# TensorE's attention work in a loop over three units, with rings of three, and the final projections of all images as a stage of their own

## The chip, the cores and the metric

The kernel runs on one core of a Trainium2 chip. The metric is device time in microseconds (us) for one execution, the median of several runs. Engines are called as in the profile: PE is TensorE (PEld its weight loads), DVE VectorE, ACT ScalarE, POOL GpSimd, SP SyncE, whose only work here is issuing DMAs. SPq and ACTq are the DMA issues of SP and ACT.

## The reference

The input x has 8 images of 56 x 56 positions with 128 channels, float32. Two residual layers follow one another: `x = x + L0(gn(x))` and `x = x + L1(gn(x))`, where gn is a group norm over 32 groups. L0 is a gated global convolution by FFT; its stages are not touched. L1 works on each position (token) by itself, with 8 heads of 16 channels:

```python
q, k, v = xs @ Wq.T, xs @ Wk.T, 2 * (xs @ Wv.T)          # each n x 8 heads x 16
q, k, v_h = l2norm(q), l2norm(k), l2norm(v)
attn_head = softmax(einsum('bnhd,bngd->bnhg', v_h, v_h))  # 8 x 8 between the heads of a token
q, k = (einsum('bnhg,bngd->bnhd', attn_head, y) for y in (q, k))
attn = softmax(einsum('bnhd,bnhe->bnde', k, q))           # 16 x 16 between channels, over heads
out = einsum('bnhd,bnde->bnhe', v, attn)
out = transpose(out, (0, 3, 1, 2)).reshape(b, n, 128) @ proj_w.T + proj_b
```

The transpose before the last product mixes tokens: row e x 196 + r of its input is channel e of all heads of tokens 16 r to 16 r + 15. So a row of the result draws on 16 tokens, and a block of results on tokens of half an image.

## The kernel before

Six stages run one after another, each a block in which every engine has its own program: load_weights, project_in, make_taps, convolve, project_out, attend. In convolve, project_in and project_out TensorE runs a hardware loop (`Fori`); the body of convolve holds 8 images with 52 matmul calls each (32, 16, 2 and 2) and some ten waits on semaphores each, and is repeated 30 times for 32 chunks. The change is in attend (L1026), whose program is written out in full on all engines.

attend handles the 25088 tokens of all images in 112 units of 224 tokens. Two units are one turn n (448 tokens, 4 blocks of 112). Its pipeline, with the names of the code:

- **SP**: load_xn (L1103) brings the normed input of turn n+3, 128 rows of 1792 B. turn (L1105 to L1118) waits until the unit four turns back has left, then loads the heads of turn n from DRAM scratch: eight DMAs into v_blocks (L1117), each of 896 runs of 32 B, and one into qk_rows (L1118), 3584 runs of 136 B. v_blocks and qk_rows have four buffers of two units each.
- **PE**, in round i: mix(i) (L1177), scores(i+1) (L1162), project of one block (L1146), outputs(i-2) (L1201), logits(i-1) (L1189), a final group if one is due (L1214, L1216), project of a second block. The projections are 8 units ahead of the attention. scores has 28 matmul calls, mix 28, outputs 28, logits 56, a projection 1, a final group 8. One float32 call shows as two matmul and two weight-load records.
- **ACT**: copy_in takes each projected block out of PSUM with two squares and a copy (L1249 to L1251); root makes the norms of a turn (L1255, square root); store_heads writes v_heads and qk_heads to scratch (L1260, 448 runs; L1261); exp_s (L1267) and exp_l (L1273) are the exponentials; leave_mix (L1281, L1282) takes mix out. Square root and exponential need different tables, so each turn has two table loads.
- **DVE**: squares and clamp (L1327, L1331), normalize_q and normalize_kv (L1341 to L1351), among them a small copy of the v norms (L1344), mask (L1358), weigh (L1364, L1369), divide (sum, reciprocal, product: L1375, L1377, L1381), leave (L1389) into oT.
- **POOL**: spreads k_mixed into k_blocks (L1136), one instruction of 1.7 us per unit.

s_exp, e_blocks, q_mixed, k_blocks, p_norm have two buffers. oT holds two images, x1_in one, ps_fin is one bank. The final projections of image b are eight groups (FINS, L1088), placed in rounds (b+1) x 14 + 3 and the seven behind it: PE adds the projection and x1 (by a product with the identity) into ps_fin, DVE adds the bias (L1397), ACT stores 196 KB (L1288) and after the eighth loads the next image's x1, 1568 KB (L1290). So 56 of the 64 groups lie within the 112 rounds, and 8 after them.

```python
            for i in range(ROUNDS):
                bk = AHEAD * BPB + 2 * i
                if unit(i):
                    mix(i)
                if unit(i + 1):
                    scores(i + 1)
```

## Time and profile before

| | before |
|---|---|
| runs | 3313.82 us median of 3 (3308.23 to 3314.02) |
| the profiled execution | 3298.07 us, its span 3296.3 us, mean clock of TensorE 0.952 |
| PE, PEld | 2941.7 us (89%), 2143.9 us (65%) |
| DVE, ACT, POOL | 1875.7 (57%), 1272.4 (39%), 565.2 us (17%) |
| DMA queue of instructions (q8) | 300 packets, 4.92 MB |
| attend | from the first load at 2011 us to the end |

The profile is of one execution. Times in the views are from the start of its span. Busy time counts an engine's instructions, not its waits; matmuls are pipelined and their ends modelled, so single durations of PE overlap and add up to more than the stretch they take, whereas the pieces of the chain don't. PEclk is the clock that TensorE was granted, as a share of full speed. Queue q1 is SP's DMAs, q10 ACT's, q8 the one that brings instructions. An idle time is given with what ended it; "issue" means nothing that the profile shows.

### The profile page before, as it was taken

Reading aid. Unit: us, or ns where it says so; the run is one execution under the profiler, and the core shown is the slowest. Engines: PE = TensorE matmul, PEld = TensorE weight load, DVE = VectorE, ACT = ScalarE, POOL = GpSimd, SP = SyncE. Lnnn points to the kernel's source line nnn. Section 1 sums busy time; section 2 is a strip of 40 time slices with the busy share of each in tenths; the row PEclk is TensorE's granted clock in tenths of the full one; section 3 lists DMA queues with packets and bytes.
Section 4 is the critical chain, followed back from the end, with each engine's and each line's share of the span. In section 5 each row is a group of like instructions: output and inputs, shape, how many; then the busy total and the mean of one; then the engine's idle time right before and its main releaser. Section 6 shows DMA issues by size and latency. Waiting matters only on the chain. (4 is left out here: it accounts for less than half of the span.)

```text
span 3296.3 us, 144029 instructions
## 1 busy us (share of the span) xinstructions
PE 2941.7 (89%) x62769; PEld 2143.9 (65%) x62769; DVE 1875.7 (57%) x3334; ACT 1272.4 (39%) x2841; POOL 565.2 (17%) x419
## 2 busy tenths in 40 slices
PE   5676989999999999999998995888898888888887
PEld 4563369766666666666665442677777777777776
DVE  4452542566666666666664774555555555556553
ACT  3553552422222222222222443554444454444431
POOL 0000030022222222222221112111111111111111
PEclk9888889999999999999999997999999999999999
DMA  5877000022112111121123994655556556555652
GB/s 140 228 231 206 1 1 1 11 47 46 45 44 46 44 45 45 44 46 44 44 46 105 412 383 139 94 85 90 99 100 109 103 89 117 92 107 85 113 87 58
DMA packets 1015825, 318.90 MB, mean 97 GB/s; under 512 B 863345, under 2 KB 1002158, under 8 KB 1010350
## 3 DMA queue, kind: packets, MB, share of 16 engines
q1 hardware_dynamic: 692626, 169.81, 24.9%
q10 hardware_dynamic: 322844, 143.73, 16.0%
q8 instruction: 300, 4.92, 0.6%
q14 instruction: 55, 0.45, 0.0%
HBM read 157.66 MB, written 155.75 MB: 95 GB/s over the span
## 5 line engine op out<-in xcount | busy, mean ns | idle before, releaser
L845 DVE TENSOR_TENSOR terms<-spec,ps_z 112x456 f32<-112x456 f32 x1024 | 575.5, 625 | 403.7 <-PE ps_z L728 403.7
L738 PEld LDWEIGHTS ps_q<-inv_w,prod 112*57 112x57 f32 x16384 | 450.9, 133 | 174.6 <-issue 172.2
L738 PE MATMUL ps_q<-inv_w,prod 112*57 112x56 f32 x16384 | 484.4, 217 | 1.3 <-DVE prod L851 1.3
L826 POOL TENSOR_TENSOR prod<-terms 112x456 f32<-112x456 f32 x256 | 297.7, 1163 | 998.8 <-DVE terms L845 998.8
L728 PE MATMUL ps_z<-x_half,fwd_w 120*112 120x456 f32 x1024 | 458.4, 570 | 0.0
L783 ACT ACTIVATE q_half<-ps_q 121x448 f32<-121x448 f32 x255 | 139.4, 547 | 826.4 <-PE ps_y L746 826.4
L1136 POOL TENSOR_TENSOR k_blocks<-k_mixed,same_of 128x896 f32<-128x896 f32 x112 | 188.2, 1680 | 1045.0 <-ACT k_mixed L1282 1045.0
L1189 PE MATMUL ps_l<-q_mixed,k_blocks 32*64 32x64 f32 x12544 | 229.6, 221 | 88.2 <-issue 87.7
L1189 PEld LDWEIGHTS ps_l<-q_mixed,k_blocks 32*64 32x64 f32 x12544 | 205.4, 133 | 106.1 <-issue 97.9
L1162 PE MATMUL ps_s<-v_blocks 128*64 128x64 f32 x6272 | 229.7, 233 | 18.7 <-issue 13.8
L1201 PEld LDWEIGHTS ps_o<-p_norm,v_blocks 128*64 128x64 f32 x6272 | 195.4, 138 | 70.4 <-issue 64.9
L728 PEld LDWEIGHTS ps_z<-x_half,fwd_w 120*112 120x112 f32 x1024 | 160.4, 176 | 121.9 <-issue 106.1
L1146 PE MATMUL ps_qkv<-weights,xn_in 128*112 128x384 f32 x448 | 212.4, 563 | 28.1 <-DMA xn_in<-x_mid_normed 16.7
L1358 DVE TENSOR_TENSOR e_blocks<-s_exp,same_of 128x896 f32<-128x896 f32 x112 | 123.6, 1104 | 193.4 <-ACT s_exp L1267 193.4
L1162 PEld LDWEIGHTS ps_s<-v_blocks 128*64 128x64 f32 x6272 | 211.4, 147 | 28.5 <-issue 16.5
L1201 PE MATMUL ps_o<-p_norm,v_blocks 128*64 128x64 f32 x6272 | 212.4, 225 | 11.3 <-issue 6.5
L1273 ACT ACTIVATE p_exp<-ps_l 128x448 f32<-128x448 f32 x112 | 61.1, 545 | 368.1 <-PE ps_l L1189 368.1
L720 PEld LDWEIGHTS ps_x<-fwd_h,v_in 56*56 56x56 f32 x8192 | 130.0, 128 | 91.8 <-issue 91.7
L1177 PEld LDWEIGHTS ps_l<-qk_rows,e_blocks 64*64 64x64 f32 x6272 | 116.2, 145 | 103.8 <-issue 99.7
L720 PE MATMUL ps_x<-fwd_h,v_in 56*56 56x57 f32 x8192 | 163.9, 218 | 4.6 <-DMA v_in<-conv_in 3.8
L851 DVE TENSOR_TENSOR prod<-terms 112x456 f32<-112x456 f32 x256 | 162.0, 633 | 8.8
L1375 DVE TENSOR_REDUCE z_sum<-p_exp 128x28 f32<-128x448 f32 x112 | 69.3, 619 | 169.4 <-ACT p_exp L1273 169.1
(135 smaller groups left out, 4315.5 us busy)
## 6 DMA issues: line engine op xcount, KB each, us to landing
qk_heads<-st_qk ACTq DMA_DIRECT2D x56, 476.0 KB, 4.2
qk_rows<-qk_heads SPq DMA_DIRECT2D x56, 476.0 KB, 6.8
conv_in<-v_sb ACTq DMA_DIRECT2D x112, 224.0 KB, 3.3
v_in<-conv_in SPq DMA_DIRECT2D x512, 49.0 KB
conv_out<-y_sb ACTq DMA_DIRECT2D x512, 49.0 KB
y<-conv_out SPq DMA_DIRECT2D x8, 1792.0 KB, 13.4
x_in<-in_x SPq DMA_DIRECT2D x8, 1568.0 KB, 9.4
shortcut<-short ACTq DMA_DIRECT2D x8, 1568.0 KB, 6.3
```

The costliest lines, as they stand in the source:

```text
L720: last = pe.matmul(ps_x[64 * ri:64 * ri + SIDE, r, c * NF:(c + 1) * NF], v_in[b % 2][rows, c * SIDE:(c + 1) * SIDE], k.fwd_h[rows, ri * NF ...
L728: last = pe.matmul(ps_z[b % 2][x][0:NFFT, 0:PC], k.fwd_w[:, x, :], x_half[b % 2][:].rearrange("p r x -> p (r x)"), start=True, stop=True)
L738: last = pe.matmul(ps_q[64 * ri:64 * ri + NF, c * SIDE:(c + 1) * SIDE], prod[b % 2][:, x, c * NF:(c + 1) * NF], k.inv_w[:, x, ri * SIDE:(r ...
L783: act.activation(q_half[:].rearrange("p c w -> p (c w)"), ps_q[0:64 + NF, 0:CC * SIDE], ACT.Copy).then_inc(q_r, 1)
L826: pool.tensor_tensor(prod[b % 2][:, 1, :], terms[b % 2][:, 2, :], terms[b % 2][:, 3, :], ALU.add).then_inc(prod_i_r, 1)
L845: last = dve.tensor_tensor(terms[b % 2][:, x, :], k.spec[0:NFFT, s, bass.ds(c * CC, CC), :].rearrange("p c f -> p (c f)"), ps_z[b % 2][z][ ...
L851: dve.tensor_tensor(prod[b % 2][:, 0, :], terms[b % 2][:, 0, :], terms[b % 2][:, 1, :], ALU.subtract).then_inc(prod_r, 1)
L1136: pool.tensor_tensor(kb[i % 2][:], bcast(km[i % 2][:], 3, 4), bcast(bcast(k.same4[:], 1, HD), 1, GU), ALU.mult).then_inc(k_r, 1)
L1146: pe.matmul((ps_b if bk % 2 else ps_a)[0:TB, 0:3 * CH], xn[n % 3][:, j * TB:(j + 1) * TB], k.w[:, WQ:WQ + 3, :].rearrange("p a c -> p (a c)"),
L1162: last = pe.matmul(to, v[:, gb, a, :], v[:, gb, a, :], start=True, stop=True)
L1189: last = pe.matmul(ps_l[half:half + 64, s // 2, g * HD:g * HD + 64], kb[i % 2][rows, g].rearrange("p d m -> p (d m)"), qm[i % 2][rows, g:g ...
L1201: last = pe.matmul(ps_o[64 * r:64 * r + 64, g * HD:g * HD + 64], vb[n % NIN][:, gb, r, :], pn[i % 2][:, a, g:g + 4, :], start=True, stop=True)
```

## The change

The unit of everything in attend is now one unit of 224 tokens instead of a turn of two for the loads: SP issues nine DMAs per unit (eight of 448 runs, one of 1792) and one load of xn, 112 KB. v_blocks, qk_rows and xn_in are rings of three units. s_exp, e_blocks, q_mixed, k_blocks and p_norm have one buffer. turn(u) waits for outputs(u-3) on PE, and its qk_rows load for leave(u-3) on DVE. TensorE's order in a round is scores(i), logits(i-1), two projections for unit i+8, mix(i), outputs(i-1). Rounds 0 to 2 are written out, rounds 3 to 101 are a loop of 33 turns with three rounds in its body, rounds 102 to 112 are written out again. The other engines' programs stay written out, in a new order. The copy of the v norms moves from DVE to POOL, with waits of root, clamp and store_heads that go with it. The output of all images stays on chip in oT (8 images). The final projections are a stage of their own, project_heads: x1 with two buffers, loaded by SP in halves, four banks of PSUM, 64 groups in a row, stores by ACT.

```diff
...
-    TB, BPB, GB, GU = 112, 4, 28, 14
+    TB, BPB, GU = 112, 4, 14
+    UT = TB * BPB // 2
...
     AHEAD = 4
-    NIN = 4
-    RPI = TOK // 16
-    RH = RPI // 2
+    AU = 2 * AHEAD
+    RING = 3
+    LOOPED = (NU - AU) // RING
...
-        xn = [sb(f"xn_in{m}", [128, BPB * TB]) for m in range(3)]
+        xn = [sb(f"xn_in{m}", [128, UT]) for m in range(RING)]
...
-        vb = [sb(f"v_blocks{m}", [128, GB, 2, 64]) for m in range(NIN)]
-        kb = [sb(f"k_blocks{m}", [128, GU, HD, 4]) for m in range(2)]
-        qk = [sb(f"qk_rows{m}", [128, GB + 1, QKW]) for m in range(NIN)]
-        ex = [sb(f"s_exp{m}", [128, GU, 64]) for m in range(2)]
-        eb = [sb(f"e_blocks{m}", [128, GU, 64]) for m in range(2)]
+        vb = [sb(f"v_blocks{m}", [128, GU, 2, 64]) for m in range(RING)]
+        qk = [sb(f"qk_rows{m}", [128, GU + 1, QKW]) for m in range(RING)]
+        ex = sb("s_exp", [128, GU, 64])
+        eb = sb("e_blocks", [128, GU, 64])
...
-        qm = [sb(f"q_mixed{m}", [128, GU + 3, HD]) for m in range(2)]
         km = [sb(f"k_mixed{m}", [128, GU, HD]) for m in range(2)]
+        qm = sb("q_mixed", [128, GU + 3, HD])
+        kb = sb("k_blocks", [128, GU, HD, 4])
...
-        oT = [sb(f"oT{m}", [128, HD, RPI]) for m in range(2)]
-        x1 = sb("x1_in", [128, TOK])
-        res = [sb(f"res{m}", [RH, 4, CH]) for m in range(4)]
-        ps_a, ps_b, ps_o, ps_f = (psum(n) for n in ("ps_qkv0", "ps_qkv1", "ps_o", "ps_fin"))
+        pn = sb("p_norm", [128, 2, GU + 3, HD])
+        ps_qkv = [psum(f"ps_qkv{m}") for m in range(2)]
+        ps_o = psum("ps_o")
...
-            def load_xn(n):
-                if n >= 3:
-                    sp.wait_ge(qkv_ps, (n - 2) * BPB)
...
-            def turn(n):
-                at = slice(n * BPB * TB, (n + 1) * BPB * TB)
...
-                if n < NIN:
+            def load_xn(w):
+                if w >= NU:
...
+                if w >= RING:
+                    sp.wait_ge(qkv_ps, 2 * (w - RING) + 2)
...
+            def turn(u):
...
+                m, n = u % RING, u // 2
+                if u < RING:
                     sp.wait_ge(cleared, m + 1)
                 else:
-                    sp.wait_ge(o_r, 2 * (n - NIN) + 2)
+                    sp.wait_ge(o_ps, u - RING + 1)
                 sp.wait_ge(st_stored[n % 2], 32 * (n // 2 + 1))
...
                 for a in range(2):
                     for q in range(4):
                         at8 = (4 * a + q) * HEADS
                         sp.dma_start(vb[m][64 * a + q:64 * a + 64:4, :, :, at8:at8 + HEADS], v[a, q]).then_inc(in_loaded[m], 16)
...
+                if u >= RING:
+                    sp.wait_ge(o_r, u - RING + 1)
+                sp.dma_start(qk[m][:, 0:GU, :], t.QK[at].rearrange("(g n) h x -> (n h) g x", n=16)).then_inc(in_loaded[m], 16)
+            for w in range(AU + 1):
+                load_xn(w)
+            for u in range(NU):
+                turn(u)
+                load_xn(u + AU + 1)
...
+            def spread_k(i):
+                pool.wait_ge(km_r, i + 1)
+                if i:
+                    pool.wait_ge(l_ps, i)
+                pool.tensor_tensor(kb[:], bcast(km[i % 2][:], 3, 4), bcast(bcast(k.same4[:], 1, HD), 1, GU), ALU.mult).then_inc(k_r, 1)
+            def copy_norm(n):
+                a = n % 2
+                pool.wait_ge(nrm_r, n + 1)
+                if n >= 2:
+                    pool.wait_ge(st_stored[a], 32 * (n // 2))
+                pool.tensor_copy(st_qk[a][:, :, :, QKM], nrm[a][:, :, 16:24]).then_inc(vn_r, 1)
...
+                spread_k(i)
+                if i % 2 == 0 and i // 2 + AHEAD - 1 < NB:
+                    copy_norm(i // 2 + AHEAD - 1)
...
+            def scores(i, m, loads):
+                pe.wait_ge(in_loaded[m], loads * 144)
...
+                    for s in range(4):
...
+            def mix(i, m):
                 pe.wait_ge(e_r, i + 1)
...
+                if not isinstance(i, int) or i:
+                    pe.wait_ge(l_exp, i)
+                pe.sem_inc(mix_seen, 1)
...
+            def outputs(u, m):
+                pe.wait_ge(p_r, u + 1)
...
+            def round_of(c, j):
+                i = c * RING + j
                 if unit(i):
-                    mix(i)
-                if unit(i + 1):
-                    scores(i + 1)
-                if bk < NB * BPB:
-                    project(bk)
-                if unit(i - 2):
-                    outputs(i - 2)
+                    scores(i, j, c + 1)
                 if unit(i - 1):
                     logits(i - 1)
-                if i in FINS:
-                    final(*FINS[i])
-                if bk < NB * BPB:
-                    project(bk + 1)
+                if unit(i + AU):
+                    for x in range(2):
+                        project(i + AU, (j + AU) % RING, c + (j + AU) // RING + 1, x)
+                if unit(i):
+                    mix(i, j)
+                if unit(i - 1):
+                    outputs(i - 1, (j - 1) % RING)
+            for w in range(AU):
+                for x in range(2):
+                    project(w, w % RING, w // RING + 1, x)
+            for j in range(RING):
+                round_of(0, j)
+            with pe.Fori(1, LOOPED) as c:
+                for j in range(RING):
+                    round_of(c, j)
+            for i in range(LOOPED * RING, NU + 1):
+                round_of(i // RING, i % RING)
...
                 act.wait_ge(nsc_r, n + 1)
+                if n >= 2:
+                    act.wait_ge(vn_r, n - 1)
+                    act.wait_ge(rn_r, n - 1)
...
                 act.wait_ge(st_r, n + 1)
+                act.wait_ge(vn_r, n + 1)
...
             def exp_s(i):
                 act.wait_ge(s_ps, i + 1)
-                if i >= 2:
-                    act.wait_ge(e_r, i - 1)
-                act.activation(ex[i % 2][:].rearrange("p (j g) x -> p j (g x)", j=2), ps_s[:, :, 0:GU // 2 * 64], ACT.Exp).then_inc(s_exp, 1)
...
+                    act.wait_ge(e_r, i)
+                act.activation(ex[:].rearrange("p (j g) x -> p j (g x)", j=2), ps_s[:, :, 0:GU // 2 * 64], ACT.Exp).then_inc(s_exp, 1)
...
-            exp_s(0)
...
+            for i in range(NU + 1):
+                if unit(i):
+                    exp_s(i)
+                if i % 2 == 0 and i and i // 2 + AHEAD - 2 < NB:
+                    store_heads(i // 2 + AHEAD - 2)
+                if unit(i - 1):
+                    exp_l(i - 1)
+                if unit(i + AU):
+                    copy_in(2 * (i + AU))
+                if unit(i):
+                    leave_mix(i)
                 if i % 2 == 0 and i // 2 + AHEAD - 1 < NB:
                     root(i // 2 + AHEAD - 1)
-                if unit(i):
...
-                if unit(i + 1):
...
-                if unit(i - 1):
-                    exp_l(i - 1)
-                if bk < NB * BPB:
...
-                if i in FINS:
-                    store(*FINS[i])
-            for m in range(4):
-                act.wait_ge(out_stored[m], 16 * 2 * BATCH)
+                if unit(i + AU):
+                    copy_in(2 * (i + AU) + 1)
...
             def clamp(n):
                 dve.wait_ge(nsq_r, 2 * n + 2)
+                if n >= 2:
+                    dve.wait_ge(nrm_r, n - 1)
...
-                dve.tensor_copy(st_qk[a][:, :, :, QKM], nrm[a][:, :, 16:24])
...
             def mask(i):
                 dve.wait_ge(s_exp, i + 1)
-                if i >= 2:
-                    dve.wait_ge(m_ps, i - 1)
-                dve.tensor_tensor(eb[i % 2][:], ex[i % 2][:], bcast(k.same8[:], 1, GU), ALU.mult).then_inc(e_r, 1)
+                if i:
+                    dve.wait_ge(m_ps, i)
...
+                if u:
+                    dve.wait_ge(o_ps, u)
+                dve.tensor_tensor(pn[:, :, 0:GU, :], pe_[a][:], bcast(zi[a][:], 3, HD), ALU.mult).then_inc(p_r, 1)
...
+            def leave(u):
+                b, r0 = u // UPI, u % UPI * GU
+                dve.wait_ge(o_ps, u + 1)
+                dve.tensor_tensor(k.oT[:, b, :, r0:r0 + GU].rearrange("p e g -> p g e"), ps_o[:, 0:GU * HD].rearrange("p (g e) -> p g e", e=HD),
+                                  qk[u % RING][:, 0:GU, QKM:QKM + 1].to_broadcast([128, GU, HD]), ALU.mult).then_inc(o_r, 1)
...
-            for i in range(ROUNDS):
+            for i in range(NU + 1):
+                if unit(i):
+                    mask(i)
+                if unit(i - 1):
+                    divide(i - 1)
                 if unit(i):
                     weigh(i)
-                if unit(i + 1):
...
-                    leave(i - 2)
                 if i // 2 + AHEAD - 1 < NB:
                     (normalize_kv if i % 2 else normalize_q)(i // 2 + AHEAD - 1)
                 if unit(i - 1):
-                    divide(i - 1)
-                if i in FINS:
-                    add_bias(*FINS[i])
-                pr = AHEAD * 2 + i
-                if pr < NB * 2:
-                    squares(pr)
-                    if pr % 2:
-                        clamp(pr // 2)
+                    leave(i - 1)
+                if unit(i + AU):
+                    squares(i + AU)
+                    if i % 2:
+                        clamp(i // 2 + AHEAD)
+            dve.wait_ge(o_r, NU)
...
+def project_heads(nc, t, k):
...
+    RPI = TOK // 16
+    RH = RPI // 2
+    NF_ = 8
...
+        x1 = [sb(f"x1_in{m}", [128, TOK]) for m in range(2)]
+        res = [sb(f"res{m}", [RH, 4, CH]) for m in range(4)]
+        ps_f = [ctx.enter_context(nc.psum_tensor(f"ps_fin{m}", [128, 512], F32)) for m in range(4)]
...
+            for b in range(BATCH):
+                if b >= 2:
+                    sp.wait_ge(f_ps, NF_ * (b - 1))
+                for h in range(2):
+                    sp.dma_start(x1[b % 2][:, h * HALF:(h + 1) * HALF], t.X1[b, :, h * HALF:(h + 1) * HALF]).then_inc(x1_loaded[b % 2], 16)
...
+            for b in range(BATCH):
+                pe.wait_ge(x1_loaded[b % 2], 32 * (b // 2 + 1))
+                for u in range(NF_):
+                    at, lo, e0 = b * NF_ + u, u // 4 * RH, u % 4 * 4
+                    if at >= 4:
+                        pe.wait_ge(f_r, at - 3)
+                    for e in range(4):
+                        to = ps_f[at % 4][0:RH, e * CH:(e + 1) * CH]
+                        pe.matmul(to, k.oT[:, b, e0 + e, lo:lo + RH], k.w[:, PW, :], start=True, stop=False)
+                        x0 = (e0 + e) * RPI + lo
+                        last = pe.matmul(to, x1[b % 2][:, x0:x0 + RH], k.ident[:], start=False, stop=True)
+                    last.then_inc(f_ps, 1)
...
+            for at in range(BATCH * NF_):
+                dve.wait_ge(f_ps, at + 1)
+                if at >= 4:
+                    dve.wait_ge(out_stored[at % 4], 16 * (at // 4))
+                dve.tensor_tensor(res[at % 4][:], ps_f[at % 4][0:RH, :].rearrange("p (e c) -> p e c", c=CH), bcast(k.proj_b[0:RH, :], 1, 4), ALU.add).then_inc(f_r, 1)
...
+            for at in range(BATCH * NF_):
...
+                act.wait_ge(f_r, at + 1)
+                rows = t.out_rows[b * TOK:(b + 1) * TOK].rearrange("(e r) c -> r e c", e=HD)
+                act.dma_start(rows[lo:lo + RH, e0:e0 + 4, :], res[at % 4][:]).then_inc(out_stored[at % 4], 16)
+            for m in range(4):
+                act.wait_ge(out_stored[m], 16 * BATCH * NF_ // 4)
...
-        attend(nc, t, k)
+        with nc.sbuf_tensor("oT", [128, BATCH, HD, TOK // 16], F32) as k.oT:
+            attend(nc, t, k)
+            project_heads(nc, t, k)
```

## Rows read from the trace of the kernel before

**Rows 1.** Busy us by stretch: length, PE, PEld, DVE, ACT, POOL, clock, DMA

```profile
1000.00:1400.00 400.00, 400.00 (x9299) 267.10 (x9296) 257.30 (x447) 110.34 (x268) 104.44 (x90) 1.00 0.19 45
2100.00:3200.00 1100.00, 969.57 (x29617) 808.83 (x29614) 640.28 (x1165) 517.98 (x1151) 169.67 (x101) 0.96 0.57 98
2502.00:2508.00 6.00, 5.56 (x128) 4.79 (x128) 3.28 (x7) 4.50 (x9) 1.03 (x1) 0.72 0.49 82
```

**Rows 2.** Waits of TensorE, 2100 to 3200 us: us in total, times, longest

```profile
PE ps_l L1189 <- issue: 78.5, 50, 3.4
```

**Rows 3.** DMA, 2100 to 3200 us: packets, MB; KB each, us to landing

```profile
q8 instruction: 234, 3.83, 1.4%
...
qk_rows<-qk_heads SPq DMA_DIRECT2D x51, 476.0 KB, 6.8
...
v_blocks<-v_heads SPq DMA_DIRECT2D x408, 28.0 KB, 4.0
...
x_in<-x_mid ACTq DMA_DIRECT2D x6, 1568.0 KB, 9.5
```

**Rows 4.** DMA queues, 800 to 1600 us: all queues that moved anything

```profile
q10 hardware_dynamic: 85204, 17.98, 10.4%
q1 hardware_dynamic: 25060, 17.98, 9.2%
```

**Rows 5.** The chain, 2480 to 2560 us: start, us, what

```profile
2513.62 0.96 PE ps_l L1177 x56
...
2524.34 1.78 PE ps_s L1162 x56
2526.12 0.83 PE ps_qkv L1146 x2
2526.95 1.78 PE ps_o L1201 x56
2528.73 1.79 PE ps_l L1189 x112
```

**Rows 6.** In order of time, around the start of attend: start, us, what

```profile
2005.05 0.33 SPq L923 DMA_DIRECT2D x_mid_normed<-xn  x1
2011.37 11.07 SPq L1103 DMA_DIRECT2D xn_in<-x_mid_normed  x4
...
2037.69 7.80 SPq L1117 DMA_DIRECT2D v_blocks<-v_heads  x8
...
2052.15 3.25 PE L1162 MATMUL ps_s<-v_blocks 128*64 128x64 f32 x56 [4.29 <-DMA qk_rows<-qk_heads]
```

**Rows 7.** In order of time, 3271 to 3293 us: final groups

```profile
3271.29 0.46 PE L1214 MATMUL ps_fin<-weights,oT 128*98 128x128 f32 x2 [0.66 <-DVE oT L1389]
...
3272.90 0.38 PE L1216 MATMUL ps_fin<-ident,x_in 128*98 128x128 f32 x2
...
3292.73 0.69 DVE L1397 TENSOR_TENSOR res<-ps_fin,proj_b 98x512 f32<-98x512 f32 x1 [2.08 <-PE ps_fin L1216]
```

**Rows 8.** In order of time, 2500 to 2535 us: one turn, one divide

```profile
2513.21 6.84 SPq L1117 DMA_DIRECT2D v_blocks<-v_heads  x8
2513.40 0.62 DVE L1375 TENSOR_REDUCE z_sum<-p_exp 128x28 f32<-128x448 f32 x1 [0.93 <-ACT p_exp L1273]
...
2514.42 0.62 DVE L1381 TENSOR_TENSOR p_norm<-p_exp,z_inv 128x448 f32<-128x448 f32 x1
```

**Rows 9.** Lines L1117 (us to landing) and L1260 (ns min/median/max)

```profile
DMA to landing us min/median/max: 3.0/4.0/9.6
...
L1260 ACTq DMA_DIRECT2D v_heads<-st_v x50: 311/312/323, 2118.9 to 3186.4; - x50
```

**Rows 10.** Groups of instructions, 2500 to 2900 us: busy us, mean ns, idle before

```profile
L1358 DVE TENSOR_TENSOR e_blocks<-s_exp,same_of 128x896 f32<-128x896 f32 x36 | 39.3, 1093 | 59.7 <-ACT s_exp L1267 59.7
...
L1267 ACT ACTIVATE s_exp<-ps_s 128x896 f32<-128x896 f32 x36 | 33.1, 918 | 29.7 <-PE ps_s L1162 29.5
...
L1267 ACT ACT_TABLE_LOAD x18 | 23.1, 1283 | 0.3
```

More of the change, by code:

```diff
@@ L1160, in scores, with logits @@
                     for a in range(2):
                         to = ps_s[64 * a:64 * a + 64, g // 7, g % 7 * 64:g % 7 * 64 + 64]
-                        last = pe.matmul(to, v[:, gb, a, :], v[:, gb, a, :], start=True, stop=True)
+                        last = pe.matmul(to, vb[m][:, g, a, :], vb[m][:, g, a, :], start=True, stop=True)
                 last.then_inc(s_ps, 1)
-            def mix(i):
-                n = i // 2
-                pe.wait_ge(e_r, i + 1)
-                if i:
-                    pe.wait_ge(q_r, i)
-                    pe.wait_ge(km_r, i)
-                if i >= 2:
-                    pe.wait_ge(l_exp, i - 1)
-                for g, gb in groups(i):
+            def logits(u):
+                pe.wait_ge(k_r, u + 1)
+                pe.wait_ge(q_r, u + 1)
+                if not isinstance(u, int) or u:
+                    pe.wait_ge(l_exp, u)
+                for g in range(GU):
+                    for s in range(4):
+                        rows, half = slice(32 * s, 32 * s + 32), 64 * (s % 2)
+                        last = pe.matmul(ps_l[half:half + 64, s // 2, g * HD:g * HD + 64], kb[rows, g].rearrange("p d m -> p (d m)"), qm[rows, g:g + 4, :],
+                                         start=True, stop=True)
+                last.then_inc(l_ps, 1)
@@ L1174, in mix @@
+            def mix(i, m):
+                pe.wait_ge(e_r, i + 1)
+                if not isinstance(i, int) or i:
+                    pe.wait_ge(l_exp, i)
+                pe.sem_inc(mix_seen, 1)
+                for g in range(GU):
                     for a in range(2):
@@ L1176, in mix @@
                         half, at = 64 * (a ^ g % 2), MC + g // 2 * QKM
-                        last = pe.matmul(ps_l[half:half + 64, g % 2, at:min(at + 64, 512)], eb[i % 2][rows, g, :], strided(qk[n % NIN][rows], gb * QKW, [[1, min(64, 512 - at)]]), start=True, stop=True)
+                        last = pe.matmul(ps_l[half:half + 64, g % 2, at:min(at + 64, 512)], eb[rows, g, :],
+                                         strided(qk[m][rows], g * QKW, [[1, min(64, 512 - at)]]), start=True, stop=True)
@@ L1178, in mix @@
                 last.then_inc(m_ps, 1)
-            def logits(i):
-                pe.wait_ge(k_r, i + 1)
-                pe.wait_ge(q_r, min(NU, i + 2))
-                pe.wait_ge(km_r, min(NU, i + 2))
-                if i:
-                    pe.wait_ge(l_exp, i)
-                for g in range(GU):
-                    for s in range(4):
-                        rows, half = slice(32 * s, 32 * s + 32), 64 * (s % 2)
-                        last = pe.matmul(ps_l[half:half + 64, s // 2, g * HD:g * HD + 64], kb[i % 2][rows, g].rearrange("p d m -> p (d m)"), qm[i % 2][rows, g:g + 4, :],
-                                         start=True, stop=True)
-                last.then_inc(l_ps, 1)
@@ L1193, in outputs @@
-            def outputs(i):
-                n = i // 2
-                pe.wait_ge(p_r, i + 1)
-                if i:
-                    pe.wait_ge(o_r, i)
-                for g, gb in groups(i):
+            def outputs(u, m):
+                pe.wait_ge(p_r, u + 1)
+                if not isinstance(u, int) or u:
+                    pe.wait_ge(o_r, u)
+                for g in range(GU):
                     for a in range(2):
                         r = a ^ g % 2
-                        last = pe.matmul(ps_o[64 * r:64 * r + 64, g * HD:g * HD + 64], vb[n % NIN][:, gb, r, :], pn[i % 2][:, a, g:g + 4, :],
+                        last = pe.matmul(ps_o[64 * r:64 * r + 64, g * HD:g * HD + 64], vb[m][:, g, r, :], pn[:, a, g:g + 4, :],
```

174 lines of the change are left out of this document (58 added, 116 removed).

## The prediction

> **What bounds the kernel now.** I read the views in this order: busy shares by stretch, what TensorE waits for, the chain, the DMA queues, then single stretches of time. The diff touches the stage attend, 2011 to 3296 us, so only that stage counts. In its middle TensorE is busy 969.57 of 1100 us, DVE 640, ACT 518, and the DMA engines 57% [rows 1]. TensorE sets the pace. But the 130 us in which it stands still are not waits for data: the largest part is "issue", 78.5 us in 50 pieces of up to 3.4 us on one line [rows 2]. The convolution, where TensorE runs a loop, has 400.00 of 400 us busy and clock 1.00; here the clock is 0.96, and it reads 0.72 in the 6 us behind one such hole [rows 1]. The instruction queue tells why: 234 packets, 3.83 MB, for 29617 + 29614 matmul and weight-load records, so 65 bytes for each record [rows 1, 3]; in 800 us of convolution that queue moved nothing [rows 4]. TensorE's written-out program is fetched while it runs, and the holes are late fetches.
>
> How long is a round without holes? The chain gives mix 0.96, scores 1.78, a projection 0.83 (two per round), outputs 1.78, logits 1.79 [rows 5]: 7.97 us. From the first scores at 2052.15 to the first of the eight bare groups at the end, at 3271.29, are 1219 us [rows 6, 7], with 112 rounds and 56 final groups in them. A final group takes 1.61 us for seven of its eight pairs [rows 7], without its first fill some 1.75 in all, 98 us for 56. (1219 - 98) / 112 = 10.0 us per round: 8.0 of work, 1.2 of holes (130 us over 101 to 112 rounds), the rest the lower clock and small waits.
>
> **TensorE in a loop.** A round has 142 matmul calls; each leaves two matmul and two load records (28 calls of scores are 56 records in [rows 5]), so three rounds are 1704 records and some 39 waits. The convolution's body is 8 images of 52 calls, 1664 records and 80 waits. By these counts the new body is no longer than one that repeats without any instruction packet. I take the fetch as gone for the 99 rounds in the loop. Rounds 0 to 2 and 102 to 111 stay written out: 13 rounds at 10.0, 130 us. Bounds for the loop: nothing, as in the convolution, or the full 10.0 of now.
> The Trainium skill speaks against the change here: Runtime: NRT & Kernel Launch, section Instruction fetch mechanics, says that a taken branch outside a two-page window forces a fetch before execution goes on, and that full unrolling is preferred. The same section gives TensorE room for 2048 instructions, by which both bodies stay inside. The trace of the convolution goes by the second statement.
>
> **The rings.** Before, a turn loads two units, four buffers deep, and TensorE never waits for it. Now turn(u) starts when outputs(u-3) are done, the last work of round u-2, and scores(u) are the first work of round u: the load has exactly one round, and logits, projections and mix stand behind its wait on TensorE. So a round lasts at least as long as a load. A full turn took 6.84 us of issues for v_blocks, and then qk_rows 6.8 from issue to landing: 13.7 [rows 3, 8]; the first turn, beside stores of ACT, took from 2037.69 to 2052.15, 14.5 [rows 6]. Half the data halves what scales, not the latency, for which I take the shortest v_blocks landing, 3.0 [rows 9]: (13.7 - 3.0) / 2 + 3.0 = 8.35, with stores 8.7, plus 0.1 of semaphores: I take 8.7 for a round. That the issues do shrink is shown by ACT's stores, 448 runs in 0.31 us [rows 9], where SP spends 0.86 on 896. Ends: all of it halves, 6.9, and the load is hidden; nothing halves, 13.7, and every round is that long. SP's other work, a 112 KB xn load after each turn, fits behind qk_rows.
> The Trainium skill, DMA: Bandwidth & Descriptors, puts a fixed cost of about 2 us on each transfer; by it the halved turn would be an estimated 7.9 us. The shortest landing here is 3.0, and I stay with it.
>
> **The new order of engines.** With one s_exp, e_blocks, p_norm and the like, work follows in one round: scores end at 1.78, exp_s 0.92, mask 1.09 [rows 10] give 3.9, before mix at 5.2. Every second round two table loads of 1.28 [rows 10] and a copy_in lie on ACT between leave_mix and the next exp_s; I take exp_s as 1.2 late from that (bounds: 0, and the 2.56 of both loads). It then runs from 3.0 to 3.9, mask ends at 5.1, and divide takes 1.64 (z_sum's start 2513.40 to p_norm's end 2515.04) [rows 8], to 6.8, where outputs could start at 6.2 (scores, logits, two projections, mix). That is 0.6 per pair of rounds, 8.3 on average, and is hidden while the load sets 8.7. The POOL copy of norms waits for the square root on ACT, with spread_k of the next round behind it, which isn't due for 5 us: nothing; were it as dear as the largest DVE item here, 1.09 every second round, POOL would still be idle half the time. The fewer DVE and POOL buffers cost nothing more for the same reason. The rounds without projections at the end stay near 8 to 10, as in the 13.
>
> **The final stage.** 56 groups leave the rounds (98 us, already out of the 10.0), and 64 now stand alone. Before it: a barrier, bounded by 0 and 6.3 us (from 2005.05, the last store of the stage before, to 2011.37 [rows 6], with that store's landing inside); I take 1.5. Then x1, 1568 KB, 9.5 to landing [rows 3], with nothing to hide it. With four banks the wait for DVE between groups goes: 64 x 1.75 = 112 us, DVE 0.69 [rows 7] hidden. One image's group of eight takes 14 us against 9.5 for its load. Straight-line fetches there: about 4 us, from 130 us of holes per 234 packets, eight packets long. The end, from the last bias at 3292.73 [rows 7] to the end of the span at 3296.3, stays at about 3.6.
>
> **Sum.** TensorE's 16 projections end at about 2048, and now scores(0) needn't wait for a full turn. 2048 + 13 x 10.0 + 99 x 8.7 + 7 (the last unit's logits to outputs) = 3046; + 1.5 + 9.5 + 112 + 4 + 3.6 = 3177 for the span, against 3296.3: 120 us less. The profiled execution was 3298.07; the median of the runs shown is 3313.82, 16 more. I take 120 from the median: 3194. Own range 3120 to 3260 (paces of 8.2 to 9.3).
>
> **Rivals.** (1) Loads faster than I think: TensorE and the odd-round divide set the pace, 8.3. 99 x 0.4 = 40 less: 3154. For it: the DMA engines are only 57% busy now, and the final traffic leaves the rounds. Against it: 8.35 even from an undisturbed turn. (2) The loop is no relief: its body doesn't stay, is fetched in every turn, and the pace remains 10.0 [rows 6, 7]. 99 x 1.3 = 129 more: 3323, since the separate stage with its bare load and barrier costs what its overlap had hidden. For it is the first of the skill's two statements; against it the queue of the convolution [rows 4]. (3) Slower by the ring: SP's eight v_blocks issues per unit hardly shrink, or landings lengthen where stores meet them. From 9.9 us a round (8.7 + 120 / 99) nothing is gained; at 10.6 it is 188 more, 3382. For it: landings of up to 9.6 us [rows 9]; against it the 0.31 us issues. Its price is paid at the wait of scores on in_loaded and nowhere else.
>
> **How the numbers follow.** Forecast 0.52, rival (1) 0.30, (2) 0.08, (3) 0.10. Within 0.2% (6.6 us, about what a measurement of this kernel can tell from no change) only the edges of (2) and (3) fall, 0.03. Faster 0.83, slower 0.14. The range 3110 to 3310 leaves out most of (2) and (3), 0.17, and a little below.
>
> **What would show it.** Right: no instruction packets between rounds 5 and 100, clock near 1.00, "issue" gone from ps_l, and in its place TensorE waiting on qk_rows at scores for about 0.7 us of a round; 64 final groups in 112 us behind a bare load of 9 to 10. Wrong: instruction packets at today's rate (rival 2); no wait on qk_rows and small ones on p_norm every second round (rival 1); waits of 2 us and more at scores, with a lower clock behind them (rival 3); final groups above 2 us, by stores or loads that can't keep up.

## The result, and the profile after

| | before | after |
|---|---|---|
| median | 3313.92 us of 4 runs (3308.23 to 3315.07) | 3556.27 us of 4 runs (3554.55 to 3567.28) |
| profiled span, clock | 3296.3 us, 0.952 | 3552.8 us, 0.913 |

The ratio is 1.0742, with a 95% interval of 1.0717 to 1.0767: 7.4% slower, where 3.6% faster was forecast, and 246 us above the range.

The page of after, its busy times and its queue of instructions (the table of before had PE 89%, and 300 packets of 4.92 MB):

```profile
PE 3015.3 (85%) x62769; PEld 2232.1 (63%) x62769; DVE 1937.6 (55%) x3276; ACT 1269.4 (36%) x2841; POOL 567.8 (16%) x473
...
q8 instruction: 372, 6.09, 0.7%
```

Busy time by stretch, as in [rows 1]; the third line is a shorter window, which lies within the loop in every kernel below:

```profile
1000.00:1400.00 400.00, 400.00 (x9300) 267.44 (x9301) 257.36 (x447) 109.88 (x267) 103.46 (x89) 1.00 0.20 45
2100.00:3200.00 1100.00, 827.91 (x24768) 696.73 (x24766) 573.88 (x919) 450.12 (x1005) 154.54 (x131) 0.86 0.43 70
2200.00:3000.00 800.00, 603.03 (x17928) 507.56 (x17923) 414.94 (x663) 324.51 (x724) 111.58 (x94) 0.85 0.42 70
```

The convolution is untouched. In attend TensorE is busy 827.91 of 1100 us instead of 969.57, at clock 0.86 instead of 0.96, with fewer matmul records: it stands still more, and works slower behind each stop. What it waits for, 2200 to 3000 us:

```profile
PE ps_s L1166 <- issue: 102.4, 39, 5.0
PE ps_o L1201 <- issue: 37.6, 36, 2.1
PE ps_s L1166 <- DMA qk_rows<-qk_heads: 33.7, 16, 5.1
PE ps_l L1177 <- issue: 22.2, 42, 1.6
```

162 us are "issue", and only 34 are the ring's load, the wait that the forecast expected. The DMA queues of the same 800 us:

```profile
q8 instruction: 189, 3.10, 1.7%
...
qk_rows<-qk_heads SPq DMA_DIRECT2D x63, 238.0 KB, 5.1
v_blocks<-v_heads SPq DMA_DIRECT2D x505, 14.0 KB, 3.0
```

There is one qk_rows load to a round, so 63 rounds in 800 us, 12.7 us each, and 189 / 63 = 3.0 instruction packets to a round, 9 to a turn of the loop. A packet is 3.10 MB / 189 = 16.4 KB; at the 65 bytes per record worked out in the prediction, one packet is about 256 instructions. **The loop's body is fetched anew in every turn.** One turn of TensorE and the head of the next, in order of time, show where it hurts:

```profile
2489.25 2.39 PE L1166 MATMUL ps_s<-v_blocks 128*64 128x64 f32 x39 [3.50 <-issue]
2492.78 1.22 PE L1166 MATMUL ps_s<-v_blocks 128*64 128x64 f32 x17 [1.14 <-issue]
2493.93 3.26 PE L1177 MATMUL ps_l<-q_mixed,k_blocks 32*64 32x64 f32 x110
2497.82 0.47 PE L1177 MATMUL ps_l<-q_mixed,k_blocks 32*64 32x64 f32 x2 [0.63 <-issue]
...
2514.77 2.84 PE L1166 MATMUL ps_s<-v_blocks 128*64 128x64 f32 x56 [1.00 <-DMA qk_rows<-qk_heads]
...
2529.15 2.39 PE L1166 MATMUL ps_s<-v_blocks 128*64 128x64 f32 x39 [3.94 <-issue]
```

At the head of each turn TensorE stands still for 3.5 to 3.9 us (the trace's record of the taken branch lasts 3.9 to 5.5 us there, and 0.21 us in the convolution). Within a turn, holes come at the same places: after 39 matmul records of scores, after 110 of logits. Each matmul has a load record of its own: from the first hole to the second are 17 + 110 matmuls, 254 records, a packet's worth. Counted over all turns, the places at which holes over 0.6 us recur lie 81, 337, 848, 1105, 1361 and 1617 recorded instructions into the body, in steps of 256 (and one of twice that). These are the borders between blocks of 256 instructions. The first lies some 80 instructions into the body (39 matmul and 39 load records, and two others), so the body starts at about place 176 of its block (place: the position within a block, 0 to 255). Its 1728 recorded instructions (1704 matmul and load records, 24 others) touch eight blocks: 176 + 1728 = 1904 = 7.4 x 256. Nine packets a turn are one more than these eight; what the ninth brings isn't shown.

The end is as forecast (in order of time):

```profile
3426.88 0.55 DVE L1367 TENSOR_TENSOR oT<-ps_o,qk_rows 128x224 f32<-128x224 f32 x1 [3.34 <-PE ps_o L1201]
3427.93 25.59 SPq L1427 DMA_DIRECT2D x_in<-x_mid  x6
3434.16 0.74 PE L1439 MATMUL ps_fin<-weights,oT 128*98 128x128 f32 x2 [7.34 <-DMA x_in<-x_mid]
```

From the last output at 3426.9 to the end of the span at 3552.8 are 126 us, against 130.6 forecast. The whole error lies in the 112 rounds: 2044.6 to 3426.9, 12.34 us each, where 130 us for 13 and 861 for 99 were forecast, 8.85 each.

### The profile page after: what moved, and what is told of

Same layout as the page of the kernel before. It is cut to its first block and busy times, and to the rows that moved or that the text cites. A ratio compares the mean times of both kernels' runs of the same rounds, so it can differ in the third digit from the quotient of the medians.

```text
span 3552.8 us, 145120 instructions
## 1 busy us (share of the span) xinstructions
PE 3015.3 (85%) x62769; PEld 2232.1 (63%) x62769; DVE 1937.6 (55%) x3276; ACT 1269.4 (36%) x2841; POOL 567.8 (16%) x473
## 5 line engine op out<-in xcount | busy, mean ns | idle before, releaser
L1166 PE MATMUL ps_s<-v_blocks 128*64 128x64 f32 x6272 | 276.6, 257 | 223.5 <-issue 162.1
L1166 PEld LDWEIGHTS ps_s<-v_blocks 128*64 128x64 f32 x6272 | 254.2, 169 | 241.1 <-issue 195.0
L1177 PE MATMUL ps_l<-q_mixed,k_blocks 32*64 32x64 f32 x12544 | 280.3, 247 | 40.1 <-issue 39.1
L1177 PEld LDWEIGHTS ps_l<-q_mixed,k_blocks 32*64 32x64 f32 x12544 | 252.5, 159 | 62.0 <-issue 50.9
L1201 PE MATMUL ps_o<-p_norm,v_blocks 128*64 128x64 f32 x6272 | 227.7, 227 | 68.7 <-issue 62.3
L1262 ACT ACTIVATE s_exp<-ps_s 128x896 f32<-128x896 f32 x112 | 102.7, 917 | 489.4 <-PE ps_s L1166 489.2
L1201 PEld LDWEIGHTS ps_o<-p_norm,v_blocks 128*64 128x64 f32 x6272 | 202.9, 140 | 84.0 <-issue 71.5
L1156 PE MATMUL ps_qkv<-weights,xn_in 128*112 128x384 f32 x448 | 188.9, 548 | 27.6 <-DMA xn_in<-x_mid_normed 15.1
L1190 PEld LDWEIGHTS ps_l<-qk_rows,e_blocks 64*64 64x64 f32 x6272 | 106.0, 138 | 75.6 <-issue 75.6
L778 ACT ACTIVATE x_half<-ps_x 120x456 f32<-120x456 f32 x256 | 142.8, 558 | 9.3 <-PE ps_x L720 9.2
## 6 DMA issues: line engine op xcount, KB each, us to landing
y<-conv_out SPq DMA_DIRECT2D x8, 1792.0 KB, 12.7
```

The lines of the kernel that those rows point to most:

```text
L778: act.activation(x_half[b % 2][:], ps_x[0:64 + SIDE, :, 0:HC * NF], ACT.Copy).then_inc(x_half_r, 1)
L1156: pe.matmul(ps_qkv[j][0:TB, 0:3 * CH], xn[m][:, j * TB:(j + 1) * TB], k.w[:, WQ:WQ + 3, :].rearrange("p a c -> p (a c)"), start=True, stop ...
L1166: last = pe.matmul(to, vb[m][:, g, a, :], vb[m][:, g, a, :], start=True, stop=True)
L1177: last = pe.matmul(ps_l[half:half + 64, s // 2, g * HD:g * HD + 64], kb[rows, g].rearrange("p d m -> p (d m)"), qm[rows, g:g + 4, :], star ...
L1201: last = pe.matmul(ps_o[64 * r:64 * r + 64, g * HD:g * HD + 64], vb[m][:, g, r, :], pn[:, a, g:g + 4, :], start=True, stop=True)
```

## The experiments

The edits are to the kernel after, except e8. **Unrolled** writes all rounds out. **Padded n** puts n increments of a semaphore that nobody reads into TensorE's program ahead of attend's first projection; they only move the loop's body to another place. **Split wait** gives qk_rows a semaphore of its own, on which mix waits, so that scores wait for v_blocks alone. Rounds and instruction packets are read as above, in 2200 to 3000 us:

| run | us | rounds in 800 us | packets |
|---|---|---|---|
| after | 3556.3 | 63 | 189 |
| e1 unrolled | 3375.9 | 75 | 169 |
| e2 padded 112 | 3265.0 | 86 | none |
| e3 split wait | 3552.7 | 63 | 191 |
| e4 padded 112, split wait | 3142.5 | 96 | 21 |
| e5 unrolled, split wait | 3319.1 | 79 | 177 |
| e6 padded 48 | 3575.4 | 63 | 189 |
| e7 padded 176 | 3373.3 | 78 | 118 |
| e8 before, its convolution padded 112 | 3514.2 | | |
| e9 split wait, padded by matmuls | 3131.8 | 95 | 24 |
| e10 padded 112, 16 smaller loads | 3635.8 | 63 | none |
| e11 unrolled, ring of four | 3336.4 | 78 | 174 |
| e12 padded 144 | 3275.7 | 86 | none |

e4 and e9 are medians of 4 runs each, the others single runs. The kernel before took 3301 to 3329 us in the same sittings, and the stages ahead of attend end up to 14 us apart between runs, so nothing is read from single runs that lie closer together than that. The packets of e4 and e9 belong to the written-out rounds at the end, which come before 3000 us there.

**Is it the loop?** e1:

```
-            with pe.Fori(1, LOOPED) as c:
-                for j in range(RING):
-                    round_of(c, j)
-            for i in range(LOOPED * RING, NU + 1):
+            for i in range(RING, NU + 1):
                 round_of(i // RING, i % RING)
```

> TensorE's 33 turns of the loop written out, all else as in the changed kernel. Two costs (theory A: the loop's taken branch, 4.2 to 5.5 us each, and the load of a unit, 11.4 us from first issue to last landing, which has one round to finish): the branch goes, but every round still has to last as long as a load, so the pace falls only from 12.3 to 11.6 to 11.9 us a round and the span to 3480 to 3510. Loop alone (theory B: without it the kernel is as before): pace 10.0, span about 3300. Load alone (theory C): no change, 3550.

Written out it takes 3375.89 us: the loop costs 180 us against straight code. But it is still 60 us above before (3315.7, beside it), so the time fits neither theory A (3480 to 3510) nor B (3300). Three rounds bring 6.8 packets (169 in 75 rounds) where the loop brings 9. TensorE now waits for the ring as well:

```profile
PE ps_s L1166 <- DMA qk_rows<-qk_heads: 80.9, 39, 3.5
PE ps_o L1201 <- issue: 28.0, 25, 2.1
PE ps_l L1177 <- issue: 27.1, 34, 1.8
```

**Is it the loop's place?** e2, and later e6, e7 and e12 with other n:

```
+            for x in range(112):
+                pe.sem_inc(pads, 1)
             for w in range(AU):
                 for x in range(2):
                     project(w, w % RING, w // RING + 1, x)
```

> 112 semaphore increments on TensorE ahead of its first projection, so that the loop's body begins elsewhere within a 256-instruction block; same body. Theory P (placement: by the places of the holes in the body a block boundary lies some 80 instructions behind its start, so that it touches eight blocks; moved by 112 it touches seven and stays): taken branches fall from 4.6 to 0.2 us, no instruction packets in the loop, and the load alone sets the pace, 11.2 to 11.5 us: span 3430 to 3460. Theory S (size: 1728 instructions are too many wherever they lie, 1713 of the convolution are not): branch 4.6 us, span 3550 as it was, plus at most 5.

The increments take some 15 us ahead of the first projection (17.4 us from the first load of xn to it, 2.1 in e1), and still the time falls from 3556 to 3264.98 us. Theory P had the cause right (no packets, branches of 0.21 us) and the time 165 us too high: it took the 11.4 us that a load lasts in after for the length of a round. Without packets beside it a load lasts 9.7 us, and two rounds share the wait for it (below). No instruction packet comes in those 800 us, and one wait is left:

```profile
PE ps_s L1166 <- DMA qk_rows<-qk_heads: 102.4, 42, 2.8
```

Two such waits and the work between them, in order of time:

```profile
2438.76 2.94 PE L1166 MATMUL ps_s<-v_blocks 128*64 128x64 f32 x56 [2.59 <-DMA qk_rows<-qk_heads]
2441.62 2.28 PE L1177 MATMUL ps_l<-q_mixed,k_blocks 32*64 32x64 f32 x112
2443.83 1.54 PE L1156 MATMUL ps_qkv<-weights,xn_in 128*112 128x384 f32 x4
2445.30 1.03 PE L1190 MATMUL ps_l<-qk_rows,e_blocks 64*64 64x64 f32 x56
2446.26 1.85 PE L1201 MATMUL ps_o<-p_norm,v_blocks 128*64 128x64 f32 x56
2447.94 1.80 PE L1166 MATMUL ps_s<-v_blocks 128*64 128x64 f32 x56
...
2458.37 2.23 PE L1166 MATMUL ps_s<-v_blocks 128*64 128x64 f32 x56 [2.63 <-DMA qk_rows<-qk_heads]
```

The same scores take 1.80 us when they follow other work and 2.94 behind the wait. The granted clock (the number before the last two) in these two stretches is 0.58 and 1.00: the idle time is paid for a second time.

```profile
2438.70:2441.70 3.00, 2.94 (x60) 2.83 (x64) 0.59 (x1) 0.00 (x0) 0.00 (x0) 0.58 0.35 21
2447.90:2449.70 1.80, 1.80 (x68) 1.73 (x64) 1.80 (x3) 0.00 (x0) 0.69 (x1) 1.00 0.02 1
```

The other places:

> The changed kernel with 48 increments in place of 112. By placement: the body's start moves from about 176 to about 224 of its 256-instruction block, so it still touches eight blocks: not kept, branches 4.6 us, 9 instruction packets a turn, span 3550 to 3570 (the increments themselves some 9 us: the 112 moved the first scores from 2045 to 2068). If the increments helped in some other way than by placement: 3265 to 3400.

> 176 increments: the body's start lies at about 96 of the next block but one, past the first 64 places, so it touches eight blocks again: not kept, span 3560 to 3600. If more padding than some 80 always helps: about 3280.

> 144 increments: the body starts 64 instructions into a block of 256 and its 1728 end with the seventh block (64 + 1728 = 1792). If a loop stays that touches seven blocks, all turns are as in the run with 112 (about 28 us, no instruction packets): 3265 + 6 for 32 more increments = 3271. If the block behind the last one is asked for too, so near the edge, turns are fetched again, wholly (3570) or every second one as with 176 (3370).

| n | start in its block | end, in blocks | packets per turn | turn |
|---|---|---|---|---|
| 0 | 176 | 7.4 | 9 | 37.8 us |
| 48 | 224 | 7.6 | 9 | 38.2 |
| 112 | 32 | 6.9 | 0 | 28.0 |
| 144 | 64 | 7.0 | 0 | 28.0 |
| 176 | 96 | 7.1 | 0 and 9, mostly in turn | 31.0 |

(Turn: mean distance of the loop's branch records. A taken branch lasts 3.9 to 5.5 us for n = 0 and 0.21 us for 112.) With n of 112 and 144 the body ends within the seventh block and stays. With 48, 3575.35 us, nothing is gained. The holes move with the body: the first recurring one lies 33 instructions in with 48 (81 - 48) and 161 in with 176 (81 - 176 + 256). With 176, 3373.28 us, the body reaches 32 instructions into an eighth block: as a rule every second turn is fetched (118 packets in 78 rounds, 4.5 per three), and takes 35 to 38 us where the others take 25 to 26. That was not expected: both theories had all turns alike. e12 was put at the very edge and came out at 3275.71 us, where 3271 was forecast for a body that stays.

**Does the convolution's loop obey the same rule?** The kernel before, with the increments in its convolution:

```
+            for x in range(112):
+                pe.sem_inc(pads, 1)
             pe.sem_inc(x_ps, 2)
             pe.wait_ge(cleared, 3)
```

> The kernel before with 112 increments on TensorE ahead of the convolution: its loop's body, 1713 instructions, begins elsewhere. Counting recorded instructions from its body to attend's, it begins at about 80 to 90 of a block now, and 79 is the last place from which 1713 fit into seven blocks; at 190 to 200 it touches eight. By placement its turn goes from 35.86 us to 40 to 43 with branches above 4 us, 30 turns: 120 to 220 more, plus 20 for the increments, span 3440 to 3540. If the convolution's loop is kept for its size: 3316 plus nothing more.

It goes from 3328.51 us (one run of the kernel before, beside it) to 3514.17: 186 us slower for 112 increments. The instruction queue in 800 to 1600 us, where [rows 4] had no packet, then the waits of that stretch, then a piece of it in order of time:

```profile
q8 instruction: 172, 2.82, 1.5%
```

```profile
PE ps_q L740 <- issue: 69.8, 39, 2.4
```

```profile
1050.43 1.09 PE L740 MATMUL ps_q<-inv_w,prod 112*57 112x56 f32 x33 [1.75 <-issue]
1053.31 1.70 PE L740 MATMUL ps_q<-inv_w,prod 112*57 112x56 f32 x30 [1.79 <-issue]
```

A turn of this loop goes from 35.86 to 41.96 us, its taken branch from 0.21 us to between 3.3 and 4.0, and 30 turns x 6.1 are 183 us. The second hole, behind 33 matmul records (66 with their loads, and three others), is the first border within the body, 69 instructions in: the body starts at about place 187 and touches eight blocks. Without the 112 it starts at about 75, and 75 + 1713 = 1788 ends four places short of the eighth block (7 x 256 = 1792). So the loop that never fetched, on which the prediction rested, had been lucky in its place.

**The ring.** e3 and e4, the split wait without and with the padding:

```
-                sp.dma_start(qk[m][:, 0:GU, :], ...).then_inc(in_loaded[m], 16)
+                sp.dma_start(qk[m][:, 0:GU, :], ...).then_inc(qk_loaded[m], 16)
...
             def scores(i, m, loads):
-                pe.wait_ge(in_loaded[m], loads * 144)
+                pe.wait_ge(in_loaded[m], loads * 128)
...
-            def mix(i, m):
+            def mix(i, m, loads):
+                pe.wait_ge(qk_loaded[m], loads * 16)
```

> qk_rows gets a semaphore of its own, and mix waits for it; scores wait for the eight v_blocks loads alone. The loop is as in the changed kernel. If the load's window is the limit in one round of three, where scores start 0.04 us behind the landing of qk_rows, that wait shrinks by the 2 to 2.5 us by which qk_rows lands later: 33 x 2.3 = 75 us, span 3470 to 3490. If the loop alone costs the time: 3550.

> Both: the body moved by 112 instructions, and scores waiting for v_blocks alone. With both costs off, a round is as long as the v_blocks load, 8.9 to 9.3 us, against 8.0 of TensorE's work: 99 x 3.2 = 315 less than the changed kernel, span 3220 to 3260, faster than the kernel before by 40 to 75 us. If placement doesn't matter (theory S): 3480, as the run with the split wait alone. If the order of the engines were a third limit, the pace would stay above 10: over 3320.

In the fetched loop the split wait is worth nothing (3552.73 us, the second of the two values expected): the 33.7 us of waiting for the load are gone, and "issue" grew from 162 to 208 us:

```profile
PE ps_s L1167 <- issue: 119.6, 49, 5.1
PE ps_o L1203 <- issue: 51.8, 42, 2.3
PE ps_l L1178 <- issue: 36.8, 59, 1.5
PE ps_s L1167 <- DMA v_blocks<-v_heads: 0.9, 2, 0.6
```

A turn still has its 9 packets and its 37.7 us: the fetch sets its length. In the loop that stays, the same edit is worth 122 us. e4 has a median of 3142.53 us (3137.2 to 3145.3), ratio to before 0.948 (0.9448 to 0.9512); the 3220 to 3260 expected took the load once more for the length of a round. Its loop ends at 2909 us. TensorE's only listed wait in 2200 to 2900 us, and its busy time there, clock 1.00:

```profile
PE ps_s L1167 <- DMA v_blocks<-v_heads: 34.7, 42, 1.2
```

```profile
2200.00:2900.00 700.00, 665.33 (x24374) 570.53 (x24372) 559.20 (x902) 441.90 (x985) 151.25 (x128) 1.00 0.62 102
```

e9 is the same kernel with the places filled by 28 one-column matmul calls (4 instructions each), two behind each of the first 14 projections:

```
+                    for y in range(2 if 2 * w + x < 14 else 0):
+                        pe.matmul(ps_s[0:64, 0, 0:1], k.w[:, WQ, 0:64], k.w[:, WQ, 0:1], start=True, stop=True)
```

> The split wait together with a loop that lies as in the run with 112 increments, but the 112 filling instructions are 28 one-column matmul calls among the first projections, where TensorE waits for ScalarE. Theory: only the place of the loop's body counts, not what fills the gap; the loop stays, turns of about 24.5 us, no instruction packets in it, and the 29 us before the first projection shrink to about 9: 3142 - 20 = 3120 (3110 to 3135). Rival, it was the increments themselves (or the later start) that helped: the loop is fetched again in each turn, 3550.

3131.80 us (3127.55 to 3138.09), ratio 0.9472 (0.9434 to 0.9509), with turns of 24.5 us as in e4. It isn't the increments that help, but the place. This is the fastest version of this study: 5.3% or 177 us below before, 425 below after. Over e4 it gains 10.7 us where 20 were forecast.

**Why a load is no faster.** e10 cuts each of the eight v_blocks DMAs in two; runs and bytes stay:

```
-                        sp.dma_start(vb[m][..., :, :, at8:at8 + HEADS], v[a, q])...
+                        for r in range(2):
+                            sp.dma_start(vb[m][..., :, r, at8:at8 + HEADS], v[a, q][:, :, r])...
```

> The padded loop without the split wait, and each v_blocks load cut into 16 DMAs of 224 runs instead of 8 of 448; bytes and runs are the same. If an issue on SP costs per DMA, whatever its runs (0.62 us each), a load's issues take 10.6 us instead of 5.3, the turn goes from 9.7 to about 15, and all 112 rounds are as long: 3265 + 112 x 5.3 = 3860. If it costs per run, nothing changes: 3265.

3635.83 us, against 3860 if an issue costs per DMA and 3265 if it costs per run. SP in order of time, e2 first and then e10:

```profile
2505.41 6.03 SPq L1112 DMA_DIRECT2D v_blocks<-v_heads  x8
2511.48 0.61 SPq L1115 DMA_DIRECT2D qk_rows<-qk_heads  x1
2512.14 1.19 SPq L1098 DMA_DIRECT2D xn_in<-x_mid_normed  x1
2513.43 5.21 SPq L1112 DMA_DIRECT2D v_blocks<-v_heads  x8
```

```profile
2508.02 11.14 SPq L1113 DMA_DIRECT2D v_blocks<-v_heads  x16
2519.21 0.60 SPq L1116 DMA_DIRECT2D qk_rows<-qk_heads  x1
2519.85 1.25 SPq L1098 DMA_DIRECT2D xn_in<-x_mid_normed  x1
2521.20 10.31 SPq L1113 DMA_DIRECT2D v_blocks<-v_heads  x16
```

An issue of a v_blocks DMA on SP costs nearly the same whatever it moves: the median distance of two is 0.70 us for 896 runs (before), 0.67 for 448 (after), 0.65 for 224 (e10). So the issues of a load took 5.1 us more (10.8 instead of 5.7 on average), about the 5.3 expected; yet a round grew only by 3.4 (9.3 to 12.7 us). The load of unit u starts when round u-2 ends, which is before round u-1 has waited for its own load. So it has that wait and the whole round u-1 to itself: with work W, load T and a mean wait w in each round, T = w + W + w, and a round is (T + W) / 2. (In e2 the waits alternate, 2.4 us in every second round and none between; their sum is the same.) For e10, T is 14.7 us from the first issue to qk_rows' landing (mean over the loop), and some 2.1 us pass before SP, still at the load before, begins; W is 565.54 us busy in 63 rounds, 9.0: (16.8 + 9.0) / 2 = 12.9, measured 12.7. For e2, T = 9.7 + 0.4 and W = 695 / 86 = 8.1: 9.1, measured 9.3.

**The straight form.** e5 is unrolled with the split wait, e11 unrolled with RING = 4:

> TensorE written out and qk_rows with its own semaphore. The written-out run waited 80.9 us of 800 on qk_rows at scores. If that wait is the ring's price and not a wait that would only move to the next fetch hole, most of it goes: 1192 us x 0.10 = 120 less than 3374, minus what v_blocks still costs: span 3260 to 3290, pace 9.6 to 9.9. If fetches take its place, as they did in the loop that is fetched anew in each turn (there the split wait changed nothing): 3350 to 3375.

> The written-out rounds with rings of four instead of three: the load has two rounds instead of one. If the 81 us of 800 that TensorE waited for qk_rows were the ring's price, they go: 75 rounds in 800 us, 1.08 per round, 112 x 1.08 = 121 less than 3376: 3255. If late fetches take their place, at most half of it goes: 3315 to 3376.

3319.05 and 3336.41 us. In e11 no wait on a load is left, but "issue" takes 149.7 us of 800 where e1 had 73.5:

```profile
PE ps_l L1177 <- issue: 62.2, 67, 1.9
PE ps_l L1190 <- issue: 29.9, 31, 2.1
PE ps_o L1201 <- issue: 28.1, 26, 2.1
PE ps_s L1166 <- issue: 27.4, 31, 1.4
```

e11 lies where late fetches were expected to take the wait's place (3315 to 3376); e5 lies between its two values. So the ring costs the written-out program only 40 to 57 of the 121 us that its waits seem to show: once it is gone, TensorE runs into late fetches sooner. Neither form is clearly faster than before: e5 is level with it (3328.51 beside it), e11 27 us above (3308.9). Only the loop in the right place is.

## Why the prediction was wrong

- **What bounds the kernel now**: right. TensorE's holes were late fetches. Where the packets are gone, so are the holes (e2, e12), and with the ring's wait gone too, the clock is 1.00 (e4).
- **"By these counts the new body is no longer than one that repeats without any instruction packet. I take the fetch as gone"**: this step failed. The count was right to within 1% (1728 recorded instructions, 15 more than the convolution's 1713); the inference was wrong, since it looked at length alone, and the same body stays or doesn't by its place. Seven blocks of 256 touched, and it stays (e2, e12, e4, e9, and the convolution in before); eight, and it is fetched in each turn (after, e6, e8), or in every second where only 32 instructions reach into the eighth (e7). Rival (2) had "no relief" at the old 10.0 us. In truth the fetched loop is worse than straight code, 12.7 us a round against 10.7 in e1, for it brings 9 packets a turn instead of 6.8 and also waits some 4 to 5 us at each taken branch. The Trainium skill, Runtime: NRT & Kernel Launch, section Instruction fetch mechanics, warned of a stall at a taken branch; the trace bears that out at 3.9 to 5.5 us where the body doesn't stay, and not where it does, 0.21 us. The same section's 2048 instructions for TensorE are eight blocks of 256: a body that touches all eight doesn't stay here. I weighed the two statements as if one had to be false.
- **"A round lasts at least as long as a load", 8.35 to 8.7 us**: wrong in size and in form. A load took 9.7 us without fetches beside it and 11.1 in e1. The issues hardly shrank (6.84 us in [rows 8], 5.2 to 6.0 in e2) where they were halved in the sum; qk_rows did shrink, from 6.8 to 3.9 us. ACT's 0.31 us for 448 runs [rows 9] was no evidence for SP: those are runs of 512 B (224 KB in all) on ACT's queue, and nothing there varied their number; on SP e10 varied it, and the cost stayed. What was missed on the other side is that the wait is shared by two rounds, (T + W) / 2. The two nearly cancel: 9.3 us measured in e2, 8.7 forecast. This was rival (3)'s mechanism, at two thirds of a microsecond instead of two.
- **The odd-round divide, 8.3 us**: the number came out, the mechanism didn't, so this was luck. In e4 and e9, where neither fetch nor qk_rows' landing holds TensorE, a turn of the loop lasts 24.5 us, 8.2 a round. But no wait on p_norm is listed in e4's loop. Its rounds are work (665.33 us busy of 700) and v_blocks' landing (34.7), 7.8 and 0.4 each.
- **The final stage**: right, 126 us against 130.6. Too long was x1's load (9.5 taken, 6.2 from issue to the first group); the 64 groups took 115 us against 112.
- **The sum**: it can be closed. 112 x (12.34 - 8.85) = 391 us more in the rounds, some 5 less at the end, 3 less before the first scores and 7 for the last unit, which the 12.34 already hold: 3177 + 391 - 15 = 3553, the span. By the runs: a body that stays is worth 3556 - 3265 = 291 us (some 306 with the increments' 15), the ring's wait on qk_rows 122. Had the place been right, the change would have come out near 3250 to 3265 us, within my range, and the split wait puts it at 3132.
- **Chances**: 0.14 for slower rested on two rivals that I priced as alternatives. They stand side by side in after, and the fetched loop's price was bounded by "the full 10.0 of now", with no end for a loop that is worse than straight code.

**Left open**: why a turn at the eighth block's edge is fetched mostly every second time, what the ninth packet of a turn is, and why the holes within a fetched turn grow when the load's wait goes (e3). Bodies of another length were not run, so seven against eight blocks is shown for 1713 and 1728 instructions alone. A larger part of the loads on another queue was not tried.

## What to carry to other kernels

A loop around a long TensorE program paid here only where its body stayed: count the instruction blocks (of 256) that it touches, its start included, not its length alone, and look in the profile for instruction packets per turn and a gap of 4 to 5 us at the turn's head. Any edit ahead of a loop can move it; where a body is near the edge, fill a place in which the engine is idle anyway, and check again after every change. And let a consumer wait only for the transfer that it reads: a semaphore shared by nine DMAs cost 122 us here.

## What was unexpected of the hardware

- 112 instructions that compute nothing took 291 us off this kernel, and added 186 us to the one before (against the one run beside it). A comparison of two versions of a kernel with long loops can measure nothing but the place.
- A body with 32 instructions in its eighth block was fetched in about every second turn.
- Transfers took longer in the runs that have instruction packets beside them; that the packets are the cause is argued, not shown. The median from issue to landing of xn_in is 4.6 or 4.7 us in after, e1, e3, e5, e6 and e11, and 3.5 or 3.6 in e2, e4, e9, e10 and e12; that of qk_rows is 5.1 us in after and 4.0 in e4. The lines of e4, 2200 to 3000 us:

```profile
qk_rows<-qk_heads SPq DMA_DIRECT2D x96, 238.0 KB, 4.0
...
xn_in<-x_mid_normed SPq DMA_DIRECT2D x87, 112.0 KB, 3.6
```

- SP pays 0.65 to 0.70 us (median) for each v_blocks DMA of 32-byte runs, whether it has 224 or 896 of them.
